# Row normalisations of a two-layer adaLN network: from VectorE scalar operations to ScalarE activations with a bias made by GpSimd

## The reference

```python
h = _layernorm(x) * (1 + ca) + sa                   # normalisation an
x = x + ga * linear_attention(h)                    # layer 0, 16 heads, elu + 1
h = _layernorm(x) * (1 + cb) + sb                   # bn1
# layer 0's expert part: normalises h again (bn3), softmax over 8 experts, the best two,
# gelu(xn @ W1[e] + b1[e]) @ W2[e] + b2[e], weighted and summed
x = x + gb * ffn(h)
h = _layernorm(x) * (1 + ca) + sa                   # cn1
x = x + ga * softmax_attention(norm(h), bias...)    # cn3; 8 heads, 512 x 512 scores
h = _layernorm(x) * (1 + cb) + sb                   # dn1, en1
x = x + gb * (h + expert_w[argmax(h @ gate_w)] applied to h)
```

## Time and profile before

| what | value |
|---|---|
| time, median of 3 runs | 837.27 us |
| lowest and highest | 828.42 and 839.52 us |
| span of the profiled execution | 708.6 us |
| PE busy | 619.4 us, 87% |
| DVE busy | 511.1 us, 72% |
| ACT busy | 385.6 us, 54% |
| POOL busy | 334.4 us, 47% |
| mean granted TensorE clock | 0.951 |

### The profile page before, as it was taken

The page is one execution under the profiler, slowest core; times in us unless marked ns, Lnnn a source line. Parts: engine busy times, 40 slices in busy tenths (PEclk is TensorE's granted clock), DMA queues, the critical chain, the costliest instruction groups (busy, mean ns, idle before and its releaser), DMA issues. The chain is left out here.

```text
span 708.6 us, 12005 instructions
## 1 busy us (share of the span) xinstructions
PE 619.4 (87%) x3832; PEld 395.1 (56%) x3832; DVE 511.1 (72%) x1298; ACT 385.6 (54%) x861; POOL 334.4 (47%) x363
## 2 busy tenths in 40 slices
PE   8996887998899979979998799968798899789974
PEld 4665556997899779958654633212233344344332
DVE  5576959447458966155887389999888665958997
ACT  2342134678967557635699377737274456366410
POOL 5112287065478577767034153754214137106934
PEclk9998999999999989999999899979898899999998
DMA  8200325588678869999944615450501616421221
GB/s 339 91 1 1 107 103 179 174 280 286 212 258 274 284 216 332 296 295 302 291 151 104 163 45 105 119 107 28 89 1 45 134 52 128 125 91 53 53 59 30
DMA packets 47421, 106.40 MB, mean 150 GB/s; under 512 B 7440, under 2 KB 22608, under 8 KB 45824
## 3 DMA queue, kind: packets, MB, share of 16 engines
q1 hardware_dynamic: 41808, 94.82, 44.9%
q0 software_dynamic: 5120, 10.50, 5.1%
q10 hardware_dynamic: 432, 0.34, 0.2%
HBM read 80.26 MB, written 25.17 MB: 149 GB/s over the span
## 5 line engine op out<-in xcount | busy, mean ns | idle before, releaser
L1359 DVE TENSOR_REDUCE mxs<-PS 128x2 f32<-128x1024 f32 x128 | 152.2, 1221 | 60.0 <-PE PS L1687 59.5
L1027 ACT ACTIVATE bufa<-PS 128x512 f32<-128x512 f32 x256 | 134.8, 608 | 63.5 <-PE PS L1713 32.1
L986 ACT ACTIVATE bufb<-PS,bufb 128x128 f32<-128x128 f32 x368 | 103.6, 376 | 69.5 <-PE PS L1652 68.4
L1652 PE MATMUL PS<-bufb 128*128 128x128 f32 x736 | 101.2, 285 | 12.6 <-DMA bufb<-in_experts_dram 10.2
L1652 PEld LDWEIGHTS PS<-bufb 128*128 128x128 f32 x736 | 93.3, 199 | 20.7 <-issue 16.3
L1660 PE MATMUL PS<-bufb 128*128 128x128 f32 x736 | 101.2, 284 | 3.0 <-ACT bufb L986 3.0
L1660 PEld LDWEIGHTS PS<-bufb 128*128 128x128 f32 x736 | 93.8, 199 | 7.2 <-ACT bufb L986 4.1
L842 POOL DMA_INDIRECT slots_in<-bufb x64 | 65.1, 1017 | 63.8 <-DVE bufb L1305 45.4
L1703 PE MATMUL PS<-stk 108*128 108x512 bf16 x256 | 87.0, 400 | 6.5 <-ACT bufa L1027 3.6
L1687 PE MATMUL PS<-stk 96*128 96x512 bf16 x256 | 80.9, 408 | 8.2 <-DVE mxs L1359 6.2
L853 POOL DMA_INDIRECT bufb<-slots_out,bufb x64 | 62.1, 971 | 50.9 <-issue 43.8
(11 more groups left out here) (302 smaller groups left out, 1031.6 us busy)
## 6 DMA issues: line engine op xcount, KB each, us to landing
bufb<-in_experts_dram SPq DMA_DIRECT2D x92, 514.0 KB, 5.2
slots_out<-bufb SPq DMA_DIRECT2D x30, 256.0 KB, 4.5
stk<-split SPq DMA_DIRECT2D x56, 128.0 KB, 7.6
bufb<-slots_in SPq DMA_DIRECT2D x25, 256.0 KB, 3.3
split<-terms SPq DMA_DIRECT2D x8, 768.0 KB, 3.8
slots_in<-hb SPq DMA_DIRECT2D x2, 1536.0 KB, 9.0
stk<-split SPq DMA_DIRECT2D x8, 384.0 KB, 4.6
X<-in_x_dram SPq DMA_DIRECT2D x4, 512.0 KB, 6.5
```

The lines of the kernel that those rows point to most:

```text
L986: last = nc.scalar.activation(hs[:, n % HR, fc, :], ps[:, P * fc:P * fc + P], ACT.Gelu_apprx_tanh, bias=ws[:, n % WR, F + fc:F + fc + 1])
L1027: nc.scalar.activation(probs[:, i % PR, j, :], psum("s2", i, j), ACT.Exp, scale=DH1 ** -0.5)\
L1359: nc.vector.tensor_reduce(mxs[:, gr % 2, 2 * j:2 * j + 2, h], psum("s1", i, j).rearrange("p (c n) -> p c n", c=2), axis=AX.X, op=ALU.max)\
L1652: last = nc.tensor.matmul(ps[:, P * fc:P * fc + P], ws[:, n % WR, P * fc:P * fc + P], xq[:, q % 2, P * x:P * x + P], start=True, stop=True)
```

## The change

The third step of all seven kinds of normalisation moves from VectorE to ScalarE. There it is an activation `Identity` with the inverse deviation as `scale` and minus the mean times the inverse deviation as `bias`, both one number per partition in SBUF. The factor that halves the sum of the two half-row means becomes -0.5, and GpSimd multiplies it by the inverse deviation in one more instruction behind each power. `bn2` is split: ScalarE's part is called `bnn`, VectorE keeps the two modulations of 128 x 1024. The next pair's statistics of a kind now wait for the normalising itself (`normed`), since the activations read the buffer that they write. In `plan()` the steps move to ACT with lengths of their own, so that the order is made anew for all engines. In the diff, `plan()` comes first (`cn2`, `cn4`, `dn2` and `dl2` move in the same way), then GpSimd's, ScalarE's and VectorE's code.

```diff
-    ('DVE', 'bn2'): 4.9, ('DVE', 'bn3'): 2.49, ('POOL', 'bn3'): 1.83, ('DVE', 'bn4'): 2.07, ('PE', 'btr'): 1.13,
+    ('DVE', 'bn2'): 2.55, ('DVE', 'bn3'): 2.49, ('POOL', 'bn3'): 1.83, ('DVE', 'bn4'): 2.07, ('PE', 'btr'): 1.13,
...
-        own_norm("an1", i, ring(i, DVE, "an2", i - 1))
-        op(DVE, "an2", i, 0, 2.2, of(POOL, "an1", i, lag=.1), ring(i, PE, "aot", i - 1), ring(i, DVE, "apr", i - 1))
-        op(POOL, "anx", i, 0, 3.0, of(DVE, "an2", i), of(DVE, "ps", 0), ring(i, POOL, "bn3", i - 1))
-        op(PE, "atr", i, 0, 1.1, of(DVE, "an2", i), take="pair")
+        own_norm("an1", i, ring(i, ACT, "an2", i - 1))
+        op(ACT, "an2", i, 0, 2.6, of(POOL, "an1", i, lag=.1), ring(i, PE, "aot", i - 1), ring(i, DVE, "apr", i - 1))
+        op(POOL, "anx", i, 0, 3.0, of(ACT, "an2", i), of(DVE, "ps", 0), ring(i, POOL, "bn3", i - 1))
+        op(PE, "atr", i, 0, 1.1, of(ACT, "an2", i), take="pair")
...
-        own_norm("bn1", i, of(DVE, "apr", i), ring(i, DVE, "bn2", i - 1))
-        op(DVE, "bn2", i, 0, 4.7, of(POOL, "bn1", i, lag=.1), ring(i == 3, PE, "apr", 3))
-        own_norm("bn3", i, of(DVE, "bn2", i), ring(i, DVE, "bn4", i - 1))
-        op(DVE, "bn4", i, 0, 2.2, of(POOL, "bn3", i, lag=.1), ring(i, PE, "btr", i - 1), ring(i, POOL, "bsc", i - 1, 3, lag=2.5))
-        op(PE, "btr", i, 0, 1.1, of(DVE, "bn4", i), take="pair")
+        own_norm("bn1", i, of(DVE, "apr", i), ring(i, ACT, "bnn", i - 1))
+        op(ACT, "bnn", i, 0, 2.6, of(POOL, "bn1", i, lag=.1), ring(i == 3, PE, "apr", 3))
+        op(DVE, "bn2", i, 0, 2.6, of(ACT, "bnn", i))
+        own_norm("bn3", i, of(DVE, "bn2", i), ring(i, ACT, "bn4", i - 1))
+        op(ACT, "bn4", i, 0, 2.2, of(POOL, "bn3", i, lag=.1), ring(i, PE, "btr", i - 1), ring(i, POOL, "bsc", i - 1, 3, lag=2.5))
...
-            own.count(nc.gpsimd.memset(scales[:, :, 0], 0.5))
+            own.count(nc.gpsimd.memset(scales[:, :, 0], -0.5))
...
-                        tt(d[:, 4 * j:4 * j + 4], d[:, 4 * j:4 * j + 4], mhalf[:, 0:4], ALU.pow).then_inc(rstd_ready[kind], 1)
-                        continue
+                        m, d = m[:, 4 * j:4 * j + 4], d[:, 4 * j:4 * j + 4]
                     if kind in OWN_NORMS:
-                        tt(d, d, mhalf[:, :], ALU.pow).then_inc(rstd_ready[kind], 1)
+                        own.link(tt(d, d, mhalf[:, 0:4] if kind == "en1" else mhalf[:, :], ALU.pow))
+                        tt(m[:, :, 0], m[:, :, 0], d, ALU.mult).then_inc(rstd_ready[kind], 1)
                         continue
...
+            def normalise(kind, i, src, dst, done, lo=0, hi=NT):
+                n = NORMS.index(kind)
+                a.wait_ge(rstd_ready[kind], i + 1)
+                for t in range(lo, hi):
+                    last = nc.scalar.activation(dst[:, t, :], src[:, t, :], ACT.Identity, bias=mom[:, n, t, 0:1],
+                                                scale=rstd[:, n, t:t + 1])
+                last.then_inc(done, 1)
...
+                if kind == "bnn":
+                    if i == PAIRS - 1:
+                        a.wait_ge(a_pr, PAIRS)
+                    if i == 1:
+                        a.wait_ge(zx, 32)
+                    normalise("bn1", i, tiles(X, i), hb[i], b_n)
...
+            normed = {"an1": a_z, "bn1": b_n, "bn3": b_z, "cn1": c_n2, "cn3": c_z, "dn1": d_z}
...
-                    v.wait_ge(rstd_ready[kind], i)
+                    v.wait_ge(normed[kind], i)
...
-                    normalise("bn1", i, tiles(X, i), h, None)
+                    v.wait_ge(b_n, i + 1)
                     v.wait_ge(s_pt, 1)
                     own.link(tt(h, h, modrow(0, i, 4), ALU.mult))
                     own.link(tt(h, h, modrow(0, i, 3), ALU.add))
...
-            def normalise(kind, i, src, dst, done, lo=0, hi=NT):
-                n = NORMS.index(kind)
-                v.wait_ge(rstd_ready[kind], i + 1)
-                if kind in OWN_NORMS:
-                    own.wait()
-                for t in range(lo, hi):
-                    last = nc.vector.tensor_scalar(dst[:, t, :], src[:, t, :], mom[:, n, t, 0:1],
-                                                   rstd[:, n, t:t + 1], ALU.subtract, ALU.mult)
```

More of the change, by code:

```diff
@@ L816, in _ @@
                     own.link(tt(d, d, epst[:, :], ALU.add))
-                    tt(d, d, mhalf[:, :], ALU.pow).then_inc(rstd_ready[kind], 1)
+                    own.link(tt(d, d, mhalf[:, :], ALU.pow))
+                    tt(m[:, :, 0], m[:, :, 0], d, ALU.mult).then_inc(rstd_ready[kind], 1)
                 if kind == "pk":
@@ L1328, in _ @@
                     stats(kind, i, tiles(X, i))
-                if kind == "cn2":
-                    if i:
-                        v.wait_ge(c_tr, i)
-                    normalise("cn1", i, tiles(X, i), Hb, c_n2)
                 if kind == "cn3":
```

85 lines of the change are left out of this document (41 added, 44 removed).

## The result

| kernel | median of 19 runs, us | lowest and highest | ratio, 95% interval |
|---|---|---|---|
| before | 832.67 | 822.8 and 839.52 | |
| changed | 834.75 | 830.26 and 842.69 | 1.0060, 1.0034 to 1.0085 |

By the ratio the change costs 0.6%, about 5 us; I had forecast 9.5 us, 1.2%. The ratio leaves out the six runs of the kernel before that lie more than 1.5% above its fastest; over all 19 runs of each kernel the medians are 2.1 us apart. The page of the changed kernel begins as follows; the second line answers to the earlier trace rows.

What follows compares the result with a forecast made beforehand. PE (87% of the span) was taken to lead, with ScalarE near full beside it or VectorE leading in some stretches. Terms 2.5 + 7 + 0 + 8 - 12 + 4 = +9.5 on 837.27 gave 847 us, range 826 to 862.

Steps and rivals of the forecast that it cites:

- The base: Whole kernel: 128.7 us of the 837.27 us time lie around the profiled span of 708.6 and stay.
- 3: 2.3: 200 to 320 us: six groups, but ScalarE mostly waits for PE's first matmuls; 0, bounds -5 and +3.
- The price of a group: Eight normalising activations on ScalarE take 2.9 us, against 2.14 undisturbed on VectorE; bounds 2.2 and 3.75.
- Terms 1 and 2: Opening to pair 0's first tile, +2.5 (0 to 7); 125 to 200 us, groups between gelus, +7 (2 to 12).
- So I hide nothing: 125 to 200 us: ScalarE at 67 of 75 us and PE at 69.3 wait for each other, so added work counts fully.
- Term 4: 320 to 410 us: `cn2 2`, `cn4 2` and four more table loads, 10.9 us, three quarters counted; +8, bounds 2 and 11.
- Term 5: 410 to 650 us: VectorE, leading, loses 15.7 us of work, four fifths counted; -12, bounds -16 and -5.
- Term 6: The end: VectorE gains sums behind `fil 3 1`, 6.2 us, less 2.4 gone ahead of it; +4, bounds -2 and +8.
- the first rival: GpSimd's queue delays powers, so ScalarE's gelus and PE's second matmuls wait; 858 us, chance 0.22.
- Covered: Rival: PE has 87% of the span and slack hides both engines' shifts; no change, 838 us, chance 0.22.
- VectorE's relief: Rival: 70 us less on VectorE count wherever it leads, and line 1138's wait goes; faster, 823 us, chance 0.11.

Runs made afterwards that it cites:

- 712 kind: Three chips on which the unchanged kernel before takes 711 to 714 us; the unedited changed kernel measured 735.16 us there (1.0313).
- 832 kind: The other chips, on which the unchanged kernel before takes 832 to 841 us; the result's comparison was made there.
- the halved activations: Changed kernel with each of the 192 normalising activations split into two of 64 columns: 786.17 us, 1.1027 to the kernel before.
- Layer 0's alone: Against the kernel before, only layer 0's normalisations on ScalarE, layer 1's staying on VectorE, with its own plan: 725.77 us (1.0195).
- layer 1's alone: Against the kernel before, only layer 1's normalisations on ScalarE, layer 0's staying on VectorE, with its own plan: 723.04 us (1.0144).

## Why the prediction was wrong, step by step

**The base.** "What lies around it, 837.27 - 708.6 = 128.7, stays" is the step that failed for the measured number. It isn't around the span, though I had said so under the profile of before as well: only 2.8 us are (831.8 and 834.6). The rest is inside, and it belongs to the chip on which the kernel was timed. With plain transfers in place of the indirect ones 135 us are gone there (840.87 and 706.13). Then the stretches that I summed over aren't those of the timed executions: where GpSimd issues its ten rows of 16 transfers, engines that I took as full stand idle for much of the time. The change meets 120 us of such pauses in the kernel before (832.67 less 712.6, the mean of three medians on the 712 kind) and 100 us in the changed one (834.75 less 735.16). By how it came about this is settled only in part: that indirect transfers make the pauses is shown, that the changed kernel loses 16 to 20 us less to them is a difference of medians or ratios (21 us on one kind, 2 to 5 on the other), and which of its waits the pauses cover stays open. By one trace of each on either kind, `s1 0` comes 82.8 us later on the 832 kind in the kernel before (403.3 and 320.4) and 67.5 in the changed one (398.4 and 330.9), so most of the difference would be there by then; but the one trace of the kernel before on that kind is the outlier.

That 834.75 lies in my range, and that the change is slower, as forecast, is luck. The change costs half of my 9.5 us or less on one kind and twice as much on the other, and where it costs 9.3 to 9.9, with plain transfers, it does so by other steps than mine.

**The sum**, on the kind of chip that the profile showed. How late the changed kernel is against the profile of before, by the starts of the named steps:

| up to | step | before | changed | late by | my term, measured | forecast |
|---|---|---|---|---|---|---|
| pair 0's first tile | `bh 0 0` | 110.3 | 110.6 | 0.3 | 1: 0.3 | 2.5 |
| 200 us | `bh 1 12` | 211.6 | 219.8 | 8.1 | 2: 7.8 | 7 |
| 320 us | `s1 0` | 320.4 | 330.9 | 10.4 | 3: 2.3 | 0 |
| 410 us | `s1 16` | 409.3 | 429.8 | 20.6 | 4: 10.1 | 8 |
| 650 us | `dx 2 0` | 651.0 | 660.8 | 9.8 | 5: -10.8 | -12 |
| the end | span | 708.6 | 729.2 | 20.6 | 6: 10.8 | 4 |

At these steps five of six terms are within 2.3 us; the sum of the misses, though, all of one sign but the first, is 11. The steps are my choice, and the split hangs on it, since the order within a stretch is new too: pair 1's first tile, which I had named as a sign (some 9 us later), is 14.0 later (189.3 and 175.3), `bh 1 4` is 5.1 and `bh 2 6` 13.8. So where one term ends and the next begins is open by some 5 us, and the agreement term by term proves less than it seems to. Half of the 21 us, besides, hangs on the indirect transfers on this kind too: with plain ones the change costs 9.3 to 9.9. Why isn't shown.

- *The price of a group*, 2.9, was low. Line 917 in the changed kernel, ns of one at least, in the median and at most, and one group in order of time:

```profile
L917 ACT ACTIVATE bufa<-X,mom,rstd x32: 477/478/494, 11.5 to 170.4; 128x128 f32<-128x128 f32 x32
```

```profile
167.67 3.19 ACT L917 ACTIVATE bufa<-X,mom,rstd 128x128 f32<-128x128 f32 x8 [1.40 <-issue]
```

  (3.19 - 0.478)/7 = 0.387 a tile. The Trainium skill, ScalarE: Activation LUTs, What ACT_TABLE_LOAD costs, gave 0.387 and 3.2 by the estimate in the prediction; the trace agrees. That groups don't stretch on ScalarE was right: all 23 take 3.17 to 3.23 in the trace of the 712 kind, while VectorE, with the same groups in the changed order, took 6.4 for `bn4 3`.

- *Terms 1 and 2.* The opening loses next to nothing, at most 0.4 us up to `bh 0 12`. Term 2 is within my bounds (2 and 12) by `bh 1 4` and `bh 1 12` and above them by `bh 1 0`. The row that answers to the earlier trace rows has `atr 1` at 49.9 and not at my 52.0:

```profile
49.91 1.91 ACT L965 ACTIVATE xTa<-PS,colm 128x256 f32<-128x256 f32 x4
```

  "So I hide nothing", said of 125 to 200, held in its effect, and the halved activations show that it holds in the opening too. Its reason didn't hold. I had ScalarE go to 67 of 75 us; it stays at 60.4, idle for 14.6 us (14.9 before), and waits 12.0 us for PE's first matmuls (11.5 before). That ScalarE still waits for PE as long as before is one of the signs by which I had called the prediction wrong. What the groups add isn't taken from ScalarE's idle time: the tiles themselves come later.
- *Term 4's size was right and its make-up wrong.* I made it of `cn2 2`, `cn4 2` and four more table loads. Layer 0's alone has neither of the two groups on ScalarE and is late by 21.9 us at `s1 16` too, layer 1's alone by 22.7, the whole by 20.6. Between `s1 0` and `s1 16` they lose 8.8, 16.1 and 10.1. So each part brings this delay by itself, and they don't add at this place. For layer 0's alone that can't be ScalarE's two groups; that it is the new order there is likely and not shown.
- *Term 5* is shown: from `s1 16` to `pvo 12` (605.6 before) the kernel wins back 11.2 us with layer 1's alone, 7.6 with the whole change and 3.7 with layer 0's alone, where VectorE keeps those steps. From `s1 16` to `dx 2 0` the changed order takes 230.9 us with ScalarE normalising and 237.9 with VectorE, and the kernel before 241.7: of the 10.8, 7 are VectorE's relief and 4 the order.
- *Term 6 failed*, in its size: +4 forecast, 10.8 measured. These are the starts of `dx 2 0` before and in the changed kernel, on the 712 kind:

```profile
650.97 1.02 PE L1756 MATMUL PS<-bufb 128*128 128x512 f32 x2
```

```profile
660.76 1.02 PE L1757 MATMUL PS<-bufb 128*128 128x512 f32 x2
```

  And these are the stretches from there to `fil 3 1` and from `fil 3 1` to VectorE's last instruction, before and then in the changed kernel; VectorE is the third busy time.

```profile
651.00:680.20 29.20, 28.22 (x122) 11.24 (x120) 27.43 (x69) 12.42 (x24) 21.26 (x22) 1.00 0.23 57
680.20:705.00 24.80, 14.92 (x40) 6.19 (x40) 22.99 (x70) 1.02 (x2) 11.12 (x13) 0.99 0.14 32
```

```profile
660.80:691.20 30.40, 29.71 (x136) 12.68 (x134) 18.70 (x59) 15.25 (x30) 18.26 (x21) 1.00 0.11 35
691.20:725.70 34.50, 18.51 (x42) 7.91 (x40) 31.60 (x72) 2.67 (x6) 22.71 (x23) 0.79 0.28 69
```

  Behind `fil 3 1` it takes 9.6 us more to the end of the span (38.0 and 28.4) where I had 6.2. VectorE's work there grows by 8.6 us. A slip of mine is part of it: by the earlier trace rows the three sums are 2.44, 2.45 and 3.4, 8.3 and not 7 to 8, so that 6.2 should have been 7.2 and the term 4.8. Ahead of `fil 3 1` I had 2.4 us "gone at least". None is gone: VectorE has 8.7 us less to do there and the stretch is 1.2 us longer, since it waits for PE, 6.08 us of it for the first half's routing (line 1746). I took work that leaves a stretch as time that leaves it.

  I looked only at VectorE's list, too, and passed over GpSimd's and SP's: the last two slot groups (`rxt`, `rdx`, `ryo`) and with them GpSimd's 16 gathers had moved behind the last pair's first half. The gathers begin at 679.2 us and not at 640.9, and `rds`, the second of which began at 670.7 before and which needs them, couldn't have kept its place. The chain of waits of the changed kernel on the 712 kind, in order of time, goes through them:

```profile
674.33 4.09 DMA slots_out<-bufb
679.20 1.08 POOL bufb L884
...
693.08 0.97 POOL bufb L884
696.57 1.21 POOL rstd L808
698.67 1.25 ACT bufb L917 x3
700.06 1.08 PE PS L1741 x4
```

  That looks like the first rival, GpSimd's queue blocking ScalarE, and by 0.9 us it is: the power for the last half begins that much behind VectorE's last statistic. ScalarE's idle time ahead of the last `dl2` is ten times as long, but nearly all of it passes before that statistic is there. VectorE, GpSimd and ScalarE in order of time:

```profile
695.51 0.16 DVE L1168 TENSOR_TENSOR rstd<-rstd,mom 128x4 f32<-128x4 f32 x1
```

```profile
696.57 1.20 POOL L808 TENSOR_TENSOR rstd<-rstd,mhalf 128x4 f32<-128x4 f32 x1
```

```profile
698.27 1.65 ACT L917 ACTIVATE bufb<-X,mom,rstd 128x128 f32<-128x128 f32 x4 [9.63 <-POOL mom L809]
```

*The rivals:* blocked by GpSimd had a price of 21 us, which is what the 712 kind measured, but by luck. `cn2 1` waited only 1.83 us, the power at the end 0.9. In all ScalarE does stand idle for 35.3 us in nine places ahead of line 917 with GpSimd as releaser, which was this rival's sign; like the 9.63 us above, such idle time holds VectorE's statistics as well, and no run splits it. Covered (838) is out on the 712 kind, by the halved activations above all, though its number is the nearest to what was measured. VectorE's relief is real (7 us from `s1 16` on) and too small.

## What to carry over

A difference between a profile's span and a median of other executions isn't time "around" the kernel until an execution has both: ask for the time of the profiled one first, and look in a second trace for stretches in which all engines but one begin far fewer instructions. When work moves between engines and a planner makes a new order, read the new list of every engine at the end of the program; a step that is costed right still moves gathers and sums that nobody costed. Work that leaves a stretch shortens it only if nothing else holds the stretch up. The idle time ahead of a step isn't what its releaser cost: compare when the releaser's own input was ready (here 0.9 us of 9.6). And an engine at 63% can be on the path with all that it does: doubling the number of its instructions tells so in one run.
